# The attention output product of a linear-attention and mixture-of-experts block, written group by group instead of summed over four groups

## The reference

```python
q_phi = sorf_phi(q, ...); k_phi = sorf_phi(k, ...)      # 32 features per head
S = jnp.einsum('chlm,chld->chmd', k_phi, v)
sum_k = jnp.sum(k_phi, axis=2)
numer = jnp.einsum('chlm,chmd->chld', q_phi, S)
denom = jnp.maximum(jnp.einsum('chlm,chm->chl', q_phi, sum_k), EPS)
out_heads = numer / denom[..., None]
```

## Time and profile before

| what | us |
|---|---|
| runs: median (lowest, highest) of 3 | 548.11 (547.3, 561.5) |
| span of the profiled execution, first to last instruction | 544.4 |
| busy: TensorE, loads | 334.3, 280.9 |
| busy: VectorE, ScalarE, GpSimd | 305.2, 206.1, 311.0 |
| L826: 256 records, mean 299 ns | 35.8 |
| L800: 256 records, mean 274 ns | 32.7 |

### The profile page before, as it was taken

One profiled execution on the slowest core, in us unless ns is written; L12 is line 12 of the kernel. 1 busy time (PEld: TensorE's weight loads), 2 busy tenths in 40 slices (PEclk: granted clock), 3 DMA queues, 4 the chain that ended last, 5 costly groups with the idle time before them and its releaser, 6 DMA issues.

```text
span 544.4 us, 10498 instructions
## 1 busy us (share of the span) xinstructions
PE 334.3 (61%) x3060; PEld 280.9 (52%) x3061; DVE 305.2 (56%) x1082; ACT 206.1 (38%) x424; POOL 311.0 (57%) x368
## 2 busy tenths in 40 slices
PE   2778999999996401437477556657467485658000
PEld 1677997987985301226355445546355364546000
DVE  4663898898777999954352324324233242234293
ACT  1497776957952001312121212122122121123194
POOL 4672866957764862454646463645455645645276
PEclk9879899999998555559779777978697888879555
DMA  6400110300302100001101010111011101111573
GB/s 166 117 1 1 43 39 1 116 0 10 108 20 58 40 0 0 0 25 35 40 20 45 29 44 19 43 34 29 29 39 39 39 24 35 45 34 37 152 229 96
DMA packets 30638, 25.60 MB, mean 47 GB/s; under 512 B 4192, under 2 KB 26288, under 8 KB 30608
## 3 DMA queue, kind: packets, MB, share of 16 engines
q1 hardware_dynamic: 26064, 15.91, 10.3%
q0 software_dynamic: 4544, 9.32, 6.1%
HBM read 16.36 MB, written 8.85 MB: 46 GB/s over the span
## 4 chain that ended last, share of the span: by engine, by line
PE 39%; DVE 21%; issue 15%; another core or an unknown queue 10%; ACT 7%; POOL 3%; DMA 2%; DVEq 1%; POOLq 0%; SPq 0%; ACTq 0%
PE bank L1024 6%; PE bank L800 4%; PE bank L1013 3%; PE bank L826 3%; PE bank L1004 3%; PE bank L1011 3%; PE bank L1028 3%; PE bank L1012 2%; PE bank L761 2%; DVE qphi L1407 2%; ACT qphi L702 2%; PE bank L1030 2%; DVE zst L1078 2%; DVE xn L1094 2%
## 5 line engine op out<-in xcount | busy, mean ns | idle before, releaser
L1407 DVE SCALAR_TENSOR_TENSOR qphi<-bank,qphi 128x512 f16<-128x512 f32 x71 | 48.9, 689 | 126.0 <-ACT qphi L702 92.9
L1024 PE MATMUL bank<-w2s,qphi 128*128 x284 | 66.3, 312 | 62.1 <-DVE qphi L1407 50.3
L702 ACT ACTIVATE qphi<-bank 128x512 f16<-128x512 f32 x71 | 42.5, 598 | 149.6 <-PE bank L1013 74.2
L513 POOL DMA_INDIRECT qphi<-xn_rows,gat_i x71 | 69.0, 972 | 25.7 <-issue 25.3
L519 POOL DMA_INDIRECT y_rows<-qphi,sca_i x71 | 70.3, 990 | 22.0 <-issue 21.7
L1024 PEld LDWEIGHTS bank<-w2s,qphi 128*128 128x128 f16 x284 | 31.3, 110 | 74.5 <-issue 67.6
L1012 PE MATMUL bank<-qphi,w1h 128*128 128x128 f16 x284 | 63.5, 240 | 4.3 <-issue 4.1
L1011 PE MATMUL bank<-qphi,w1h 128*128 128x128 f16 x284 | 64.2, 242 | 2.9 <-issue 2.9
L1013 PE MATMUL bank<-qphi,w1l 128*128 128x128 f16 x284 | 63.2, 239 | 2.6 <-issue 2.6
L1028 PE MATMUL bank<-w2s,qphi 128*128 x284 | 60.9, 244 | 0.0
L510 POOL TENSOR_TENSOR carrier<-mhalf 1x1 f32<-1x1 f32 x40 | 7.3, 183 | 79.1 <-DVE qphi L1416 44.2
(11 more groups left out here) (190 smaller groups left out, 902.7 us busy)
## 6 DMA issues: line engine op xcount, KB each, us to landing
stage<-in_w SPq DMA_DIRECT2D x16, 256.0 KB, 2.8
xn_rows<-hl SPq DMA_DIRECT2D x8, 256.0 KB, 3.0
kphi<-y_rows SPq DMA_DIRECT2D x8, 256.0 KB, 3.4
w2s<-y_rows SPq DMA_DIRECT2D x8, 256.0 KB, 3.6
out<-w2s SPq DMA_DIRECT2D x8, 256.0 KB, 2.3
qphi<-xn_rows,gat_i POOLq DMA_INDIRECT x71
y_rows<-qphi,sca_i POOLq DMA_INDIRECT x71
x_sb<-in_x SPq DMA_DIRECT2D x1, 512.0 KB, 3.7
```

What stands on the lines that cost most here:

```text
L513: pool.indirect_dma_start(out=xg[:, i + j, :], out_offset=None, in_=xn_d, in_offset=bass.IndirectOffsetOnAxis(ap=gat_i[:, i + j:i + j + 1] ...
L702: act.activation(hid_h[:, (i - 1) % 2, :], H_BANK[(i - 1) % 2][:, :], ACT.Relu)\
L1024: pe.matmul(dst[:, 0:2 * E], hid_h[:, q, P * c:P * c + P], both, start=(c == 0), stop=False, skip_group_check=True)
L1407: dve.scalar_tensor_tensor(out=hid_l[:, 1 - q, :], in0=H_BANK[1 - q][:, :], scalar=0.0, in1=hid_h[:, 1 - q, :], op0=ALU.max, op1=ALU.subtr ...
```

## The change

`s_sb` shrinks to 4 x 36 columns, side by side, and its memset goes. Each of the four products of a tile streams only the 36 columns of its group and writes them to their own place in the bank, each with start and stop set; nothing is added across groups. The number of matmuls and of loads stays.

```diff
-        s_sb = sb("s_sb", [P, NG * (NG + 1) * W])
+        s_sb = sb("s_sb", [P, NG * W])
...
-            pool.memset(s_sb[:, :], 0.0)
...
                     for g in range(NG):
-                        ins = pe.matmul(PHI_BANK[n % 2][:, NG * W * i:NG * W * i + NG * W],
-                                        qphi[:, g, P * t:P * t + P], s_sb[:, NG * W * g:NG * W * g + NG * W],
-                                        start=(g == 0), stop=(g == NG - 1))
+                        at = NG * W * i + W * g
+                        ins = pe.matmul(PHI_BANK[n % 2][:, at:at + W], qphi[:, g, P * t:P * t + P],
+                                        s_sb[:, W * g:W * g + W], start=True, stop=True, skip_group_check=True)
...
-                dve.tensor_tensor(s_sb[:, :].rearrange("p (g w) -> p g w", g=NG)[:, :, 0:W],
+                dve.tensor_tensor(s_sb[:, :].rearrange("p (g w) -> p g w", g=NG),
                                   S_BANK[:, 0:NG * W].rearrange("p (g w) -> p g w", g=NG),
                                   bc(sm_sb[:, :], 1, NG), ALU.mult).then_inc(S.s_ready, 1)
```

## The result

The changed kernel takes 575.9 us (median of 4, 573.6 to 584.1), the kernel before 549.0 in the same comparison: ratio 1.048, interval 1.044 to 1.051, or 26.9 us more.

A forecast was written before the change was run, and what follows sets the result against it. A chain through stages bounds the kernel, no engine being busy over 61%. Clock falls of 5.0 + 6.8 + 6.8 + 6.8 = +25.4 us on 548.1 give 573.5 us; forecast's own range 562 to 580, overall range 546.4 to 579.

The forecast's parts named there:

- The clock falls in every burst: L826 bursts, samples 0 to 3: TensorE drops to 1.2 GHz until the projections' dense work, +25.4 us; chance 0.64.
- The price at 1.2 GHz: TensorE after a fall: a load-bound 32-bit record takes 211 ns, a 16-bit one of 128 columns 106 ns.
- By sample: Clock loss in the attention part: +5.0 us in sample 0 and +6.8 us in each of samples 1 to 3.
- the price of sample 1: Sample 1 from 92.2 us: TensorE ends at 111.8 instead of 104.3, +7.5, plus 0.5, less 1.2 for waits: +6.8 us.
- VectorE's slack used up: Divisions in samples 1 and 2: TensorE's slack of a little under 2 us is counted inside the clock sum.
- The columns at 2.4 GHz: L826 at full clock: 109 instead of 126 ns a record, 17 ns saved, 1.0 us in all.
- the case where the clock holds: Rival for the bursts: 2.4 GHz stays, 1.0 us saved, 547.1 us (543.7 to 548.5); chance 0.24.
- The memset's 0.7 us: GpSimd at 1.75 us (L321): 0.70 us of work goes, hidden by VectorE's wait for x; taken as 0.
- The rule weighed: TensorE's bursts: by the skill's rule a gapless burst keeps its clock; the prediction held the trace against it.
- the first rival: L826 bursts: the clock holds at 2.4 GHz, not slower, 547.1 us; chance 0.24.

The follow-up runs named there:

- the second profile: The changed kernel unedited, profiled again: span 580.9 us; lower executions 583.0 and 584.3 us against 553.2 to 561.2 of the kernel before.
- the first profile: The changed kernel's own page, from its 584.1 us execution, which also spent the sums of sample 0 at 1.2 GHz.

## Why the prediction was right

**The clock falls in every burst.** Forecast at 0.64, and so it was: four falls, 1.3, 3.3, 1.5 and 1.0 us after the burst's start in the second profile. Predicted +25.4 and 573.5 us, measured +26.9 and 575.9. That columns are the cause, and not the form, is shown by 144 columns restored, and by the kernels in which the width alone differs from sample to sample.

**The price at 1.2 GHz.** 211 ns a 32-bit record, measured 209. This term carried nearly the whole sum.

**By sample.** 5.0, 6.8, 6.8, 6.8 predicted; 5.4, 4.8, 7.9, 8.2 measured, the last with the projection's own growth. That the sum came out within 1 us of 26.4 is in part luck: sample 1 lies 2.0 below its term, the others together 2.9 above theirs.

Sample 1 came cheaper in that execution because its clock fell late, 3.3 us into the burst, when its first half was nearly done; where it fell 1.5 us into it, in the kernel with only samples 1 and 2 narrow, it was +6.3.

Sample 2 got the price of sample 1 because it runs the same loop body, and there the term was mis-sized. It holds 1.2 us taken off for TensorE's own later waits, 0.77 of them before the projection at 111.23. The same projection of sample 2 before, in the timeline, has no wait:

```profile
148.22 1.14 PE L838 MATMUL bank<-wo_sb,attT 128*128 128x128 f32 x8
```

From burst to burst TensorE has 1.3 us of waits in sample 1 before that are gone where samples 1 and 2 alone are narrow; in sample 2 it has 0.3 us of such waits. With 0.3 taken off instead of 1.2 the term would be 7.7; measured 7.9.

In sample 3 the clock fell 1.0 us into the burst where the sum had 1.5, and it stayed down through the last projection; where it fell 1.4 us into the burst and was back before that projection (narrow in sample 3 only), the price was +6.9.

**VectorE's slack used up.** Before, VectorE never waited for L826 in sample 1. In the second profile of the changed kernel (90 to 125 us; who waited for whom, us in total, times, longest) it does, and its statistics wait for the projection:

```profile
DVE den L1136 <- PE bank L826: 1.8, 2, 1.6
DVE zst L1077 <- PE bank L837: 1.6, 1, 1.6
```

**The columns at 2.4 GHz.** This term was mis-sized too: 109 ns a record, measured 112 to 114, so 12 to 14 ns saved, not 17. And of the 1.0 us that I gave the case where the clock holds, 0.2 us was there: from first burst to last projection 117.2 us with 108 columns, 117.4 before. TensorE now waits for VectorE's division instead, 0.36 us in sample 1 and 0.41 in sample 3 of that profile. It carried nothing of the forecast.

**The rest.** The memset's 0.7 us had no effect that the runs show: the first burst of the changed kernel starts at 55.02 us in the second profile, no earlier than the 53.82 before. It wasn't tested by itself. From the end of the last projection to the end of the span the changed kernel needs as long as before: 582.0 less 209.3 in the page of the changed kernel, 544.4 less 172.4 before: 372.7 and 372.0 us.

**The rule weighed.** The Trainium skill has TensorE lose its clock when it stands idle between bursts of matmuls (TensorE: Matmul & The Clock Gate, "Why this matters for your kernels"). By it the time would have been the first rival's, 547. The traces don't agree: in sample 1 of the second profile the clock fell 3.3 us into a burst without a wait, and the last two waits before this burst, 0.75 and 0.61 us, are those of the kernel before (0.74 and 0.61), whose clock stayed. And TensorE was busy for 99.6% or more of each of the four low stretches of the first profile.

What stays open: how much must stream for the clock to hold. 36 columns fell in every burst of the changed kernel. 72 fell in samples 0 and 3 and held in 1 and 2. 108 and 144 fell for 3.4 us at most, in some profiles, and again in sample 0 or 3. So where a burst falls in the sequence mattered too; no run changed that by itself.

## What to carry to other kernels

Where the load of the stationary tile sets TensorE's pace, cutting the moving columns saves little (here 12 to 14 ns of 126 a record), and it can cost the clock: then the records behind it on TensorE take nearly twice as long (here 209 ns instead of 112). Read the granted clock over each stage before and after, and ask of a stage that is all loads whether its columns could be made wider for free, with surplus results that the next product overwrites or nobody reads. Where single executions of a kernel lie well above its lowest, look there for the same cause in another stage.

## What the runs showed of the hardware that I had not expected

- A TensorE that is busy 100% of a stretch can be granted 1.2 GHz throughout it (27.2 us of sums with 36 columns), where the same program with 96 columns gets 2.4 GHz.
- Columns of zeros kept the clock: 108 of the 144 columns of the kernel before were zeros.
- The same kernel before took 465 to 468 us in its lower executions on two chips and 553 to 561 on a third, while sample 0 with 144 columns took 37.0 us from burst to burst in the sets of both kinds that have a profile of it.
